# A decoder block with causal attention: the six output products of a head, split in two around the next head's last scores

## The reference, cut to what matters

```python
q = rope((x @ Wq.T).reshape(B, L, 32, 64)); k = rope((x @ Wk.T).reshape(B, L, 8, 64)); v = (x @ Wv.T)...
attn = einsum('bkgqd,bkld->bkgql', qh, kh) * 64 ** -0.5      # causal mask, softmax over l
out = einsum('bkgql,bkld->bkgqd', p, vh)                     # 32 heads side by side: width 2048
x = layernorm(x + out @ Wo.T)
x = layernorm(x + quantized_expert(x, fside, ctx))
x = layernorm(x + ffn(x))                                    # signs of the weights, relu, 2048 wide
```

## Time and profile before

| | |
|---|---|
| median of 3 runs | 1414.03 us (1411.48 to 1414.09) |
| the profiled execution | 1410.46 us |
| its span in the trace | 1408.6 us |
| busy share, matmuls of TensorE | 92% |
| weight loads of TensorE | 76% |
| VectorE, ScalarE, GpSimd | 72%, 64%, 56% |
| granted TensorE clock, mean | 0.981 of full speed |

### The profile page before, as it was taken

How to read it: one execution, slowest core, us unless ns; L and a number is a source line. 1 busy time by engine, 2 the same in 40 slices (tenths; PEclk the granted TensorE clock), 3 DMA queues, 4 the chain that set the end, 5 groups by cost and what they waited for, 6 DMA issues and landing times.

```text
span 1408.6 us, 25177 instructions
## 1 busy us (share of the span) xinstructions
PE 1293.1 (92%) x7101; PEld 1075.5 (76%) x7112; DVE 1012.7 (72%) x2491; ACT 904.2 (64%) x2140; POOL 783.6 (56%) x686
## 2 busy tenths in 40 slices
PE   3699999999999999989999999899998898999996
PEld 2578888887888877878887788788776675878784
DVE  3476777777777776888987888778896788965322
ACT  2477667677767776766775766677767764565332
POOL 3555565556555576545764557476661263746453
PEclk9899999999999999999999999999999998999998
DMA  4422222222222223233222222322223602100000
GB/s 176 151 68 71 76 52 60 52 65 54 69 62 71 71 59 90 83 90 83 61 69 61 68 61 53 91 54 68 54 60 121 239 16 75 45 16 30 1 30 30
DMA packets 54853, 98.78 MB, mean 70 GB/s; under 512 B 11744, under 2 KB 13792, under 8 KB 53728
## 3 DMA queue, kind: packets, MB, share of 16 engines
q1 hardware_dynamic: 54752, 97.57, 24.8%
HBM read 51.39 MB, written 4.19 MB: 39 GB/s over the span
## 4 chain that ended last, share of the span: by engine, by line
PE 75%; DVE 9%; ACT 6%; issue 5%; POOL 3%; DMA 1%; ACTq 0%; DVEq 0%; SPq 0%; POOLq 0%
PE m L1828 30%; PE ps_s L1828 9%; PE ps_o L1885 8%; PE m L2105 7%; PE ps_t L1873 7%; PE ps_s L2119 4%; PE ps_t L2119 3%; DVE pT_lo L1538 2%; PE m L1895 2%; ACT pT_hi L1265 2%; ACT probs L1257 1%; DVE o_sum L1490 1%; PE pc L1984 1%; DVE probs L1476 1%; POOL o_lo L1087 1%
## 5 line engine op out<-in xcount | busy, mean ns | idle before, releaser
L1257 ACT ACTIVATE probs<-probs,neg_max 128x128 f32<-128x128 f32 (+3 forms) x512 | 285.3, 559 | 151.8 <-DVE neg_max L1476 151.2
L1538 DVE TENSOR_TENSOR pT_lo<-ps_t,pT_hi 128x512 fp32r<-128x512 f32 (+1 forms) x384 | 220.7, 595 | 143.4 <-ACT pT_hi L1265 141.2
L1476 DVE CUSTOM_DVE_ANT_0 probs<-ps_s,mask 128x128 f32<-128x128 f32 (+3 forms) x512 | 228.2, 482 | 6.6 <-PE ps_s L1828 6.6
L1828 PE MATMUL ps_s<-k_st,q_st 128*128 128x256 f32 (+2 forms) x1024 | 232.3, 349 | 0.4 <-DVE neg_max L1476 0.4
L1873 PE MATMUL ps_t<-ident,probs 128*128 128x128 f32 x1280 | 185.5, 276 | 49.1 <-DVE pT_lo L1538 34.8
L1873 PEld LDWEIGHTS ps_t<-ident,probs 128*128 128x128 f32 x1280 | 146.8, 141 | 74.5 <-DVE pT_lo L1538 44.6
L1265 ACT ACTIVATE pT_hi<-ps_t 128x512 fp32r<-128x512 f32 (+1 forms) x384 | 186.1, 519 | 11.9 <-PE ps_t L1873 8.9
L1087 POOL TENSOR_TENSOR o_lo<-o_sum,o_hi 128x512 fp32r<-128x512 f32 x64 | 81.8, 1279 | 195.0 <-ACT o_hi L1279 194.9
L1885 PE MATMUL ps_o<-pT_hi,v_st 128*128 128x256 f32 (+2 forms) x512 | 168.7, 340 | 0.2 <-DVE o_sum L1484 0.2
L1136 POOL TENSOR_TENSOR hid_lo<-hid,hid_hi 128x512 fp32r<-128x512 f32 x64 | 83.0, 1297 | 133.7 <-ACT hid_hi L1441 133.6
L1885 PE MATMUL ps_o<-pT_lo,v_st 128*128 128x256 f32 (+2 forms) x512 | 155.4, 325 | 0.0
(11 more groups left out here) (249 smaller groups left out, 3064.9 us busy)
## 6 DMA issues: line engine op xcount, KB each, us to landing
q_st<-q_tmp SPq DMA_DIRECT2D x512, 64.0 KB, 2.0
raw<-in_wq_t SPq DMA_DIRECT2D x32, 256.0 KB, 3.0
k_st<-k_st SPq DMA_DIRECT2D x64, 128.0 KB, 2.4
raw<-in_wo_t SPq DMA_DIRECT2D x32, 256.0 KB, 2.9
raw_b<-in_ffn_t SPq DMA_DIRECT2D x10, 512.0 KB, 6.8
y<-in_x_t SPq DMA_DIRECT2D x4, 1024.0 KB, 10.5
raw<-in_wkv_t SPq DMA_DIRECT2D x16, 256.0 KB, 3.8
y<-in_x SPq DMA_DIRECT2D x4, 1024.0 KB, 5.9
```

Of the source, the lines that this page charges most:

```text
L1257: act.activation(probs[:, h % 2, SO[i]:SO[i] + SW[i]], probs[:, h % 2, SO[i]:SO[i] + SW[i]], ACT.Exp, bias=neg_max[:, h % 2, i:i + 1], sca ...
L1476: dve.tensor_tensor_reduce(out=probs[:, h % 2, SO[i]:SO[i] + SW[i]], in0=ps_s[:, i % 2, 0:SW[i]], in1=mask[:, L - SW[i]:L], scale=-SCALE, ...
L1538: dve.tensor_tensor(pT_lo[:, d, :], ps_t[:, (h + k) % 2, 0:P * w].rearrange("p (w c) -> p w c", c=P), f32(pT_hi[:, d, :]), ALU.subtract).t ...
L1828: i = pe.matmul(dst, a, c, start=(j == 0), stop=(j == len(terms) - 1))
```

## The change

`project_out` gets a parameter that says which pair's three matmuls it issues. The wait for the bank (`m1_read`) and for the operands (`o_los`) stands before the first pair, the signal `m1_full` behind the second. The calls at the middle of a head issue the first pair where all six stood, and the second pair behind `scores` 2 and 3 of the next head. The calls elsewhere (`out0` of (1,1), `out3 early`, the last ones) keep all six together.

```diff
-            def project_out(idx, u, buf, i):
-                pe.wait_ge(m1_read, idx - 1)
-                pe.wait_ge(o_los, (u + 1) * 2)
+            def project_out(idx, u, buf, i, pairs=(0, 1)):
+                if 0 in pairs:
+                    pe.wait_ge(m1_read, idx - 1)
+                    pe.wait_ge(o_los, (u + 1) * 2)
                 d = slice(P * i, P * (i + 1))
-                terms = []
-                for p in range(2):
-                    terms += split_terms(o_hi[:, buf, p, d], o_lo[:, buf, p, d], woT_hi[:, p, :], woT_lo[:, p, :])
-                product(m1[:, :], terms).then_inc(m1_full, 1)
+                for p in pairs:
+                    terms = split_terms(o_hi[:, buf, p, d], o_lo[:, buf, p, d], woT_hi[:, p, :], woT_lo[:, p, :])
+                    for j, (a, c) in enumerate(terms):
+                        last = pe.matmul(m1[:, :], a, c, start=(p == 0 and j == 0), stop=(p == 1 and j == 2))
+                if 1 in pairs:
+                    last.then_inc(m1_full, 1)
...
+                        out = None
                         if h == 0 and b != 1 and prev:
-                            project_out(m1_fill(g, b, "out3"), u - 2, b % 2, 3)
+                            out = (m1_fill(g, b, "out3"), u - 2, b % 2, 3)
                         if h > 0 and prev and (b, h) != (1, 1):
-                            project_out(m1_fill(g, b, f"out{h - 1}"), u - 1, (b + 1) % 2, h - 1)
+                            out = (m1_fill(g, b, f"out{h - 1}"), u - 1, (b + 1) % 2, h - 1)
+                        if out:
+                            project_out(*out, (0,))
                         if half == 1:
                             later("pe2", slot(g, b, h))
                         transpose_probs(n, h, 2)
                         if more:
                             scores(*ahead, 2)
                             scores(*ahead, 3)
+                        if out:
+                            project_out(*out, (1,))
```

## The result

The changed kernel takes 1432.26 us (median of 4 runs, 1430.08 to 1432.88), the kernel before 1412.76 us (4 runs, 1410.12 to 1414.09). The ratio is 1.0139 (95% interval 1.0123 to 1.0154): 19.5 us slower. The forecast was 1437 us, 23 us slower, range 1426 to 1443.

A forecast was written before the change was run, and what follows sets the result against it. TensorE was taken to set the pace, idling 3% of the time in attention. Losses read head by head gave 24.9 us, 23.4 without step 15, taken as 23: 1414.03 + 23 = 1437 us, range 1426 to 1443.

The forecast's parts named there:

- The wait that is uncovered: Before a head's last transposes, TensorE newly waits for the first group's evacuation: 0.16 us in (6,0,0), 0.33 in (6,0,2).
- The tie of the scores to the maxima: Behind the last transposes, scores 2 wait for VectorE's first maxima: 0.08 us more per head.
- The second pair covers nothing: Behind the scores, the three moved products take 0.69 us and cover no wait, since the projection starts at once.
- The later signal: m1_full comes 1.3 us later, at some 4.2 us, hidden because its reader add_y starts 5.46 us into the head.
- What could give it back: Earlier scores might shorten the next head's wait for exponentials, but ScalarE's queue has no gap: nothing given back.
- The sum: Losses over 91 mid-head products, 65 of them losing: 24.9 us, 23.4 without step 15, taken as 23.
- The forecast let the clock add nothing: The new waits are short, and with waits up to 0.68 us step 6 keeps clock 1.00: nothing added.
- No change, because TensorE has slack: TensorE isn't the pace, with weight loads busy 76%, so waits are absorbed: 1414 us; chance 4%.
- Faster, by earlier exponentials: Scores 2 and 3 come 0.5 us earlier, removing waits for probs at head starts: 1404 to 1412 us; chance 3%.
- Slower by half: VectorE's long stretches absorb much of steps 8 to 14, 9.7 us falling to 3: 1430 us; chance 18%.
- the likeliest case: The new waits are paid as read head by head: 1437 us, own range 1432 to 1442; chance 75%.

The follow-up runs named there:

- Experiments 2 to 4: Kernel before with six, one and two of a mid-head product's six matmuls moved behind the next head's scores: ratios 1.0483, 1.0006 and 1.0050.
- 5 and 6: ScalarE's o_part copy put behind the first pT_hi, in the changed kernel (1423.51 us) and in the kernel before (1420.18 us).
- experiment 5: The changed kernel with ScalarE's o_part copy put behind the first pT_hi: 1423.51 us, ratio 1.0081.
- Experiment 10: Kernel before with ScalarE's q_tmp copies of heads (0,1) and (1,1) put behind the last two exponentials: 1433.95 us, ratio 1.0157.
- the cover in (1,1) alone: Kernel before with the four short transposes of the values put in front of the last transposes of heads (1,1): 1402.97 us, ratio 0.9952.
- both covers: Kernel before with four projection matmuls in heads (1,0) and four short value transposes in (1,1) put before the last transposes: 1406.48 us.
- (1,0)'s cover alone: Kernel before with four projection matmuls put in front of the last transposes of heads (1,0): 1411.43 us, ratio 1.0005.

## Why the prediction was right, point by point

*The wait that is uncovered* was right to the hundredth. Forecast were transposes at 2.19 us and no bracket in (6,0,0), 2.41 us in (6,0,2); measured were 2.19, and 2.41 with a bracket of 0.18. The evacuation itself stayed where it was, its end 2.13 us into (6,0,0). Experiments 2 to 4 show that it is the evacuation's place, by the 2.19 us without cover and by the bend in the price; 5 and 6 show it by moving that place: some 16 of 19.5 us went, and 9.5 of 11.3 in steps 0 to 6.

*The tie of the scores to the maxima,* 0.08 us, showed as 444.94 − 444.74 = 0.20 us between transposes and scores, where the earlier trace rows has 0.13; experiment 5, with the wait nearly gone, kept 0.06 us. In both the scores start 0.06 to 0.07 us behind the end of the first maxima, but the maxima moved together with the evacuation, and I didn't test them as the cause by themselves.

*The second pair covers nothing.* Right: 445.86 to 446.54 is added in front of the projection, and nothing behind it starts earlier. The later signal was hidden, as forecast: `add_y` starts 5.46 us into (6,0,0) in both kernels.

*What could give it back.* The waits for `probs` went from 14.3 us only to 13.4. That ScalarE's queue is the whole chain there was too simple. Experiment 10 took the copies out of it, and the maxima held the exponentials at the same place; the two were level.

*The sum* was 3.5 us too large, 3.9 against the 23.4 us read head by head. The time of 1437 us was 4.7 us too high; the other 1.3 us is the kernel before, which with a fourth run had a median of 1412.76 instead of 1414.03 us. By steps, from the starts of the first heads in both traces: steps 0 to 5 9.8 us forecast, 9.8 measured; step 6 1.46 and 1.49 (it lasts 63.31 us before and 64.80 after; the 63 and 64.5 of the forecast are those of the window of the earlier trace rows, which is 0.3 us shorter than the step); steps 6 and 7 3.9 and 3.3; steps 8 to 14 9.7 and 7.2; step 15 nothing and 0.1; the first head started 0.85 us earlier in the profiled execution after, 0.64 of it by a shorter wait for the first loads, which no edit explains. The term that was mis-sized is steps 8 to 14, and more than half of what it lacks is one head. (10,1,1) isn't edited and became 1.4 us shorter. Its stretch in the kernel before and in the changed one (length, busy times, then clock, DMA share, GB/s):

```profile
740.66:752.65 11.99, 8.83 (x38) 7.09 (x37) 9.25 (x19) 6.43 (x17) 6.89 (x7) 0.72 0.28 61
```

```profile
756.22:766.77 10.55, 7.37 (x38) 5.92 (x37) 8.73 (x17) 6.43 (x17) 6.39 (x7) 0.84 0.24 54
```

The wait in it is the same, 3.16 and 3.18 us, but the granted clock is 0.72 in one and 0.84 in the other: it came back to full speed sooner. The forecast let the clock add nothing, and for the new waits that held; this was an old one. The part missing in step 7, 0.5 us, is in (7,0,2) and (7,1,2), whose transposes already came 0.2 us late before the change. I counted the distance of their starts as cover.

*The rivals.* "No change, because TensorE has slack" is refuted: each 0.1 us of uncovered wait was paid in full in steps 0 to 6. The rule of the Trainium skill (Perfetto Trace Analysis, Identifying the Most-Contended Engine), that weight-load busy share, beside the share of peak arithmetic, tells the headroom, didn't tell it here for the first of the two: 76% left no room in the heads that this change lengthens. The trace agrees with its other half, that matmul busy share is a poor measure: that share counted some 11.5 of 19.5 us of new waiting as work. "Faster, by earlier exponentials" needed the waits for `probs` to fall by 10 us; they fell by 0.9. "Slower by half" was closest to the time, 1430 against 1437 us, and level with the likeliest case in the difference (16 and 23 us, measured 19.5), but not for its reason: VectorE's long stretches absorbed little; steps 8 to 14 still paid 7.2 us.

## What to carry to other kernels

Work that stands between a producer and the reuse of its buffer is cover, and its worth is a threshold: find the place at which the buffer comes free (here 2.19 to 2.41 us into the heads of step 6), and what can be moved away is what stands beyond it. One product was free and three were not. Where a wait is filled with other work, look at what the neighbour then meets too early; of two covers the one that shortened its head by 0.92 us had 0.6 taken back by its neighbour, and the one that shortened it by 0.3 us hardly anything, so in steps 0 to 7 they were worth the same, 2.8 and 2.5 us. In the whole time they were worth nothing and 6.8 us; what set them apart lies in three heads with long waits and in the clock of the last step. A small edit is judged stage by stage, with the clock beside it.

## What the runs showed of the hardware, unexpected

*Two views of one wait.* For the same added waiting of 19.5 us, the matmuls' waits for the evacuation rose by 8.0 us, and the weight loads' from 44.6 to 81.8 us, by 37.2. The first hides what fits behind a modelled end, the second counts time in which matmuls still ran. Only distances between starts gave the sum.

*A clock that fell or didn't with like waits.* In step 15, the heads (15,0,2) and (15,0,3) hold waits of 1.8 and 1.9 us for VectorE's `y` in all kernels with six products in place. In the kernel with the cover in (1,1) alone, and in the one with both covers, the stretch of these two heads reads

```profile
1049.68:1067.11 17.43, 13.78 (x93) 11.73 (x92) 11.89 (x32) 11.13 (x28) 1.89 (x2) 1.00 0.69 201
```

```profile
1048.02:1068.18 20.16, 16.50 (x92) 14.11 (x91) 12.08 (x32) 11.29 (x28) 1.88 (x2) 0.86 0.67 199
```

The same work took 2.7 us longer at a granted clock of 0.86, that is, partly at 1.2 GHz. By the starts, counted from the span's start, the kernel with both covers was 9.5 us ahead of the kernel before at the start of step 15 and 4.8 us ahead at its last head; (1,0)'s cover alone was 5.0 ahead and ended level. So the clock of this step is why the cover in (1,0) was worth nothing in its profiled execution. Of the fourteen profiled executions, five show 1.00 in all of (15,0,0) to (15,1,2), the kernel before and the changed one among them; the other nine fall to 0.83 or 0.84 in one or more of these heads, and their step 15 is 1.6 to 4.9 us longer. The 19.5 us of the change aren't touched by it, but differences of a few us between the experiments are. Why it fell in some kernels and not in others, with waits alike, I can't say from these runs.
